# Macaron block, both gates: the normalization moves from VectorE to ScalarE, two batches ahead

## The reference

```python
x = x + 0.5 * ffn(layernorm(x))
x = x + attn(layernorm(x))
x = x + 0.5 * ffn(layernorm(x))

def ffn(x):                                   # E = 8 experts, K = 2
    logits = einsum('bsd,de->bse', x, gate_w) + gate_b
    probs = softmax(logits, axis=1)           # over the 512 tokens of a batch
    vals, idx = top_k(probs, 2)
    h = relu(x @ w1[e] + b1[e]); h = relu(h @ w2[e] + b2[e]); y = relu(h @ w3[e] + b3[e])
    v = einsum('ebso,bse->eo', y, w_tok)      # one vector for each expert
    return einsum('bse,eo->bso', indicator, v)
```

## Time and profile before

| | |
|---|---|
| median of 3 runs | 1137.03 us (1135.55 to 1138.68) |
| the profiled execution | 1137.88 us, of which the span from first to last instruction is 1136.1 us |
| PE busy | 1051.9 us, 93% of the span |
| DVE busy | 834.8 us, 73% |
| POOL busy | 696.8 us, 61% |
| ACT busy | 571.3 us, 50% |
| transfers | 59.35 MB, mean 52 GB/s |

### The profile page before, as it was taken

One profiled execution on the slowest core, in us unless ns is written; L12 is line 12 of the kernel. 1 busy time (PEld: TensorE's weight loads), 2 busy tenths in 40 slices (PEclk: granted clock), 3 DMA queues, 4 the chain that ended last, 5 costly groups with the idle time before them and its releaser, 6 DMA issues.

```text
span 1136.1 us, 15486 instructions
## 1 busy us (share of the span) xinstructions
PE 1051.9 (93%) x5687; PEld 636.9 (56%) x5687; DVE 834.8 (73%) x1078; ACT 571.3 (50%) x771; POOL 696.8 (61%) x367
## 2 busy tenths in 40 slices
PE   4599998679999999999999999999999976699996
PEld 1478886346555555555645654655654523588883
DVE  9979997757766766766766766776774464799994
ACT  3245555336554654644644654654564533255551
POOL 3435666357775776775785786686587662166552
PEclk8689999779999999999999999999999987699998
DMA  5143330000010011001001001001001112333312
GB/s 153 60 167 130 127 114 1 19 1 20 21 39 20 20 39 22 20 21 39 21 21 39 21 21 39 20 21 38 22 20 32 29 39 63 108 129 120 124 56 74
DMA packets 36336, 59.35 MB, mean 52 GB/s; under 512 B 10501, under 2 KB 23846, under 8 KB 36262
## 3 DMA queue, kind: packets, MB, share of 16 engines
q1 hardware_dynamic: 36262, 58.37, 17.0%
HBM read 55.20 MB, written 2.62 MB: 51 GB/s over the span
## 4 chain that ended last, share of the span: by engine, by line
PE 87%; DVE 9%; POOL 2%; issue 1%; ACT 1%; DMA 0%; SPq 0%; ACTq 0%; POOLq 0%; DVEq 0%
PE ring L745 19%; PE ring L516 8%; PE ring L510 8%; PE ring L512 8%; PE ring L698 6%; PE ring L716 5%; PE ring L722 5%; PE ring L718 5%; PE ring L720 5%; PE ring L755 5%; PE ring L731 3%; DVE xn L1048 2%; PE ring L680 2%; PE ring L655 1%; PE ring L681 1%; PE ring L682 1%
## 5 line engine op out<-in xcount | busy, mean ns | idle before, releaser
L1219 DVE TENSOR_REDUCE mx<-ring 128x2 f32<-128x1024 f32 x256 | 299.6, 1226 | 90.5 <-PE ring L698 90.5
L429 POOL TENSOR_TENSOR sum_picksT<-sum_picksT,P_wb 128x1024 f32<-128x1024 f32 x128 | 324.6, 2536 | 18.3
L916 ACT ACTIVATE P_wb<-ring 128x1024 f32<-128x1024 f32 x256 | 262.3, 1027 | 66.5 <-PE ring L722 38.2
L429 POOL TENSOR_TENSOR sum_picksT<-P_wb 128x1024 f32<-128x1024 f32 x64 | 153.9, 2404 | 175.0 <-ACT P_wb L916 175.0
L469 POOL TENSOR_TENSOR R<-t,R 128x512 fp32r<-128x512 f32 x128 | 163.6, 1300 | 145.5 <-ACT R L841 145.5
L745 PE MATMUL ring<-P_wb,t 128*64 128x512 f32 x1024 | 226.8, 595 | 0.0
L745 PEld LDWEIGHTS ring<-P_wb,t 128*64 128x64 f32 x1024 | 70.4, 137 | 133.0 <-issue 128.5
L836 ACT ACTIVATE t<-ring,bcol 128x512 f32<-128x512 f32 x128 | 81.4, 685 | 122.9 <-PE ring L516 120.0
L928 ACT COPY OZ<-ring 128x512 f32<-128x512 f32 x64 | 37.0, 588 | 198.8 <-PE ring L745 156.5
L698 PE MATMUL ring<-R 64*128 64x512 f32 x512 | 107.7, 416 | 6.0 <-DVE mx L1219 3.8
L510 PE MATMUL ring<-R,whi 128*128 128x512 f32 x320 | 105.8, 412 | 5.9 <-DVE ring L1160 3.2
(11 more groups left out here) (147 smaller groups left out, 1392.8 us busy)
## 6 DMA issues: line engine op xcount, KB each, us to landing
P_wb<-wd SPq DMA_DIRECT2D x64, 512.0 KB, 3.7
rzb_indp<-rzd SPq DMA_DIRECT2D x64, 256.0 KB, 3.9
xs<-in_L_attn_x SPq DMA_DIRECT2D x8, 256.0 KB, 3.8
zrc<-SZ SPq DMA_DIRECT2D x128, 2.0 KB, 1.7
out<-xs SPq DMA_DIRECT2D x8, 256.0 KB, 2.5
sum_picksT<-in_L_ffn_w SPq DMA_DIRECT2D x2, 512.0 KB, 5.3
MR<-mT SPq DMA_DIRECT2D x64, 4.0 KB
t<-in_L_ffn_w SPq DMA_DIRECT2D x1, 512.0 KB, 7.2
```

The lines of the kernel that those rows point to most:

```text
L429: pool.tensor_tensor(US[:, g % 2, c, :, :], first, PU[:, TPB * c + t, :, :], ALU.add).then_inc(s_ua, 1)
L916: act.activation(PU[:, u, :, :], ring[slot(("scores", g, u))][:, :, :], ACT.Exp, scale=SCALE).then_inc(s_exp, 1)
L1219: dve.tensor_reduce(mx[:, :, u], ring[slot(("max", g, u))][:, :, :], AX.X, ALU.max).then_inc(s_max, 1)
```

## The change

- DVE's `normal` goes to ACT: `Identity(scale * x + bias)` with `rstd` as scale and a new column `nmr` = -mean * rstd as bias, one instruction for a tile. In ACT's order the tiles of batch b+1 stand ahead of the two copies of batch b.
- `invert` gets one more small DVE operation, which writes `nmr`: six times in the program, twice in each gate and twice in attention, where `invert` is used too (for batch 0, and for batches 1 to 7).
- ACT rounds the three weight matrices into `whi`.
- POOL zeroes `MR`, ahead of its wait for the turned biases.
- Everything else stands as before. Attention's own `x_normal` stays on DVE.

```diff
+        nmr = sb("nmr", [P, NT])
...
@@ gpsimd
+            pool.memset(MR[:, :, :, :].rearrange("p g c s -> p (g c s)").bitcast(F32), 0.0).then_inc(s_mrz, 1)
             pool.wait_ge(s_bt, 1)
             pads()
             gate(0)
@@ scalar
             def gate(f):
                 s = F[f]
+                normals = [0]
+
+                def normal(b):
+                    act.wait_ge(s_nmr, (1 if b < TPB else 2) if f == 0 else (5 if b < B - 1 else 6))
+                    wait(act, s["xn_transposed"], b - 1)
+                    for j in range(TPB):
+                        t = TPB * b + j
+                        act.activation(xn[:, b % 2, j, :], xs[:, t, :], ACT.Identity, bias=nmr[:, t:t + 1],
+                                       scale=rstd[:, t:t + 1]).then_inc(s["xn_done"], 1)
+
                 for stage, arg in gate_steps(f):
                     if stage == "turn":
+                        for nb in range(normals[0], min(arg + 2, TPB if f == 0 and arg < TPB else (B - 1 if f and arg < B - 1 else B))):
+                            normal(nb)
+                            normals[0] = nb + 1
                         act.wait_ge(s["xn_transposed"], arg + 1)
...
+                    elif stage == "weights":
+                        act.wait_ge(s_wf, 64)
+                        act.copy(whi[:, arg, :, :].rearrange("p e o -> p (e o)"), wraw[arg]).then_inc(s_whd, 1)
@@ vector
             dve.memset(lgs, 0.0)
-            dve.memset(MR[:, :, :, :].rearrange("p g c s -> p (g c s)").bitcast(F32), 0.0)
             dve.memset(NEG[:, :].bitcast(F32), 0.0).then_inc(s_zero, 1)
...
             def invert(k):
                 dve.wait_ge(s_std, k + 1)
-                ln_link(dve.reciprocal(rstd[:, PARTS[k]], std[:, PARTS[k]]))
+                t = PARTS[k]
+                ln_link(dve.reciprocal(rstd[:, t], std[:, t]))
+                dve.scalar_tensor_tensor(out=nmr[:, t], in0=mean[:, t], scalar=-1.0, in1=rstd[:, t], op0=ALU.mult, op1=ALU.mult
+                                         ).then_inc(s_nmr, 1)
...
-                def normal(b):
-                    wait(dve, s["xn_transposed"], b - 1)
-                    for j in range(TPB):
-                        t = TPB * b + j
-                        dve.tensor_scalar(xn[:, b % 2, j, :], xs[:, t, :], mean[:, t:t + 1], rstd[:, t:t + 1],
-                                          ALU.subtract, ALU.mult).then_inc(s["xn_done"], 1)
...
-                    elif stage == "turn":
-                        normal(arg)
...
                     elif stage == "weights":
-                        dve.wait_ge(s_wf, 64)
-                        dve.tensor_copy(whi[:, arg, :, :].rearrange("p e o -> p (e o)"), wraw[arg]).then_inc(s_whd, 1)
                         if arg == 2:
```

More of the change, by code:

```diff
@@ L204, in macaron_kernel @@
         s_pads = sem("pads_zeroed")
+        s_nmr = sem("shift_ready")
+        s_mrz = sem("max_rows_zeroed")
         s_u, s_uc = sem("update_added"), sem("update_copied")
```

## The result

The changed kernel takes 1143.4 us (median of 4 runs, 1142.8 to 1144.9), and the kernel before 1137.3 us on the same chip (4 runs, 1135.6 to 1138.7): a ratio of 1.0065 with an interval of 1.0052 to 1.0078. **The change costs 0.65%**: that is 7.4 us (5.9 to 8.9). The medians lie 6.1 us apart, or 0.54%, within that interval. The profiled execution took 1142.83 us with a span of 1141.0 us, 4.9 us over the span before.

A forecast was written before the change was run, and what follows sets the result against it. PE carried 87% of the chain, but in the gates DVE was on it, slowed by POOL. Terms 3.0 + 0.75 + 1.2 - 0.1 + 0.2 = 5.05, rounded to 5.1 us, took the median from 1137.03 to 1142.1 us; range 1136.4 to 1146.5.

The forecast's parts named there:

- The tile on ACT: Both gates: one normalization on ACT lasts 0.48 us, 0.38 us from start to start in a row.
- The rival that it is free: Both gates: a column of scales costs nothing, 0.29 us a tile, 1136.5 us, no change; chance 0.15.
- deeper pipelining: Both gates: tiles in a row overlap more, below 0.30 us each, so the kernel gains, to 1133 us; chance 0.13.
- no overlap: Both gates: ACT's tile instructions do not overlap, 0.48 us a tile, +6.3 us, 1148.4 us; chance 0.06.
- In line with the copies: Second gate, batches 0 to 6: ACT's tiles and copies stand in line, 2.49 us a batch, +3.0 us.
- a wait for PE between batches: Gates: ACT was to have no other engine to wait for in steady state; such waits would make the prediction wrong.
- Batch 7: Second gate, last batch alone on the chain: `nmr` and four tiles take 1.62 us, not 1.11, +0.75 us.
- The first gate: First gate: ACT's last copy ends 2.0 us later, part is given back at POOL's subtractions, +1.2 us.
- The clock rival: Second gate: PE's clock stays at 1.2 GHz into the output projection, +4 to +7 us, 1146 to 1149 us; chance 0.06.
- what the cover gives back: End of first gate: DVE was waiting for POOL anyway, so a +2.0 us delay shrinks to +1.1, at most 1.4.
- The start, POOL's zeroing, the casts: Start of kernel and ACT's casts: statistics end earlier but POOL's paddings still hold DVE, casts cost nothing; -0.1, 0 to -0.5 us.
- `nmr` in attention: Attention's start: `nmr` for batch 0 stands between root and normalization, +0.2 us; hidden for batches 1 to 7.

The follow-up runs named there:

- e4: Changed kernel with scale=1.0 in place of the column `rstd` in ACT's tiles, so tokens are shifted and not scaled; 1138.5 us, 1.0017 of the kernel before.
- e1: Changed kernel with the first gate's normalizations back on DVE, the second gate's still on ACT; 1142.4 us, 1.0052 of the kernel before.
- e10: Changed kernel with `nmr` allocated behind all other tiles; 1144.8 us, 1.0068 of the kernel before.
- e2: Changed kernel with the second gate's normalizations back on DVE, the first gate's still on ACT; 1140.2 us, 1.0035 of the kernel before.
- e3: Changed kernel with every normalization on DVE and no `nmr` operation, keeping ACT's casts and POOL's memset; 1137.3 us, 1.0009 of the kernel before.
- e12: Changed kernel with all normalizations on DVE and `nmr` not allocated, keeping ACT's casts and POOL's memset; 1135.3 us, 0.9987 of the kernel before.

## Why the prediction was right, and where not

- **The tile on ACT** (0.48 us each, 0.38 from start to start): measured 0.484 and 0.387. e4 shows that the unknown part, the column of scales, costs 90 ns where 91 were taken. The rival that it is free falls, and so do those of deeper pipelining and of no overlap. The Trainium skill (ScalarE: Activation LUTs, What ACT_TABLE_LOAD costs), from whose figures the estimate of 0.386 us from tile to tile was worked out, agrees with the trace (0.387).
- **In line with the copies** (2.49 us a batch): measured 2.49. In the second gate +3.37 us where +3.0 was forecast: ACT worked from 926.44 to 944.34 us with one pause of 0.17, so 17.9 us where 17.55 were forecast; 28 tiles at 0.387 and not 0.38 us are 0.2 of the difference and the pause is the rest. The prediction had named a wait for PE between batches as a sign of being wrong. There was this one, of 0.17 us in seven batches, and e1 and e10 have it too: it needed a term, but it does not set the pace. e1 repeats the stretch to 0.01 us. Shown.
- **Batch 7** (+0.75): from the table load to PE's turn of the tiles 2.91 us before and 3.64 after, +0.73.
- **The first gate** (+1.2, with the start's -0.1): +2.52 in this pair. This term was mis-sized, in three steps. ACT's last copy ended at 35.5 us and not 33.9, mostly by the first: the second `nmr` was costed at 0.2 us and took 1.22, because it met POOL, though the prediction names this effect for three other operations, so ACT began the second root's tiles at 22.9 us and not 21.8:

```profile
20.31 2.51 POOL L456 TENSOR_TENSOR R<-OT_xnT,R 128x512 fp32r<-128x512 f32 x2 [1.23 <-ACT OT_xnT L876]
...
21.63 1.22 DVE L1053 SCALAR_TENSOR_TENSOR nmr<-mean,rstd 128x16 f32<-128x16 f32 x1
...
22.89 3.18 ACT L863 ACTIVATE xn<-xs,nmr,rstd 128x128 f32<-128x128 f32 x8 [1.58 <-DVE nmr L1053]
```

- The second step is PE's clock, to which the prediction gave no term in this gate. The turn of batch 7 took 1.11 us and not the 0.66 of full clock, and ACT waited 0.26 us for it. From the last copy to the successor of L1123 the forecast kept 3.0 us and it took 3.8, since the four logits took 2.98 us, and 2.02 at full clock, before and in the second gate. The stretches of the changed kernel, then of before (from:to, length, busy time and count of PE, PEld, DVE, ACT and POOL, the granted clock, DMA share, GB/s):

```profile
24.00:28.00 4.00, 2.24 (x10) 1.02 (x10) 0.39 (x3) 4.00 (x11) 0.90 (x1) 0.86 0.00 0
28.00:32.00 4.00, 3.41 (x7) 0.76 (x6) 0.00 (x0) 3.97 (x9) 1.63 (x2) 0.50 0.01 2
32.00:36.00 4.00, 3.29 (x10) 1.21 (x9) 0.00 (x0) 3.74 (x9) 1.73 (x2) 0.50 0.00 0
```

```profile
28.00:32.00 4.00, 3.26 (x12) 1.10 (x12) 4.00 (x11) 3.05 (x7) 1.44 (x2) 0.84 0.00 0
32.00:36.00 4.00, 2.87 (x19) 1.94 (x18) 3.33 (x5) 0.00 (x0) 4.00 (x3) 1.00 0.00 0
```

- From 28 us on ACT is busy nearly 4.00 of 4 us and DVE not at all, which is the mechanism in one row; and PE is still at 1.2 GHz (0.50) in a stretch in which it was back at 2.4 GHz (1.00) before. **The clock rival** was right in kind in the first gate, for about 1 us here, and wrong where it was placed, in the second gate: the clock came back later there too (0.50 at 930 to 934 us, 0.95 before), but behind ACT's pace that cost nothing, and it was at 1.00 when the projection began.
- The clock could cost more. In e2 and e10, which have the same tiles on ACT in the first gate, it stayed at 0.50 until past 40 us, and the product of W2 and b1 took 3.5 us and not 1.9. The changed kernel, then e10:

```profile
37.27 1.95 PE L610 MATMUL ring<-bcol,sum_picksT 128*128 128x1 f32 x16
```

```profile
36.99 3.58 PE L610 MATMUL ring<-bcol,sum_picksT 128*128 128x1 f32 x16
```

- The third step is what the cover gives back. The delay is +4.35 us at L1123's successor (39.25 against 34.90 us) and +2.5 at the gate's end, so 1.8 us came back, of which the forecast expected 0.9. The forecast was that POOL's third subtraction would hold L1079 or L1080 until 42.6 us. It ended at 43.95 us, as those two only began, and held neither: L1080 had taken 2.35 us before and takes 0.29 now (L1094), while the scaling of the probabilities, held by the second subtraction, went from 1.65 to 2.20 us (L1077).
- e2 and e10 show how much of this is chance. Both had L1123's successor at 40.61 us, +5.7 us. In e2 the scaling then took 0.49 us and the gate ended at 63.12, +2.63 us; in e10 it took 2.85 us and the gate ended at 65.50. That the first gate costs time on ACT is shown by the medians: e2 at +0.35% against e3 at +0.09% on the same chip, some 3 us with about 1.8 to each side. The 2.5 us of this pair of traces are one outcome of several.
- **The start, POOL's zeroing, the casts** (-0.1, 0 to -0.5): e3 is at +0.09% and e12 at -0.13%, both about nothing. The first root came at 10.35 us and not earlier than the 10.21 before, because two small operations (L1034, L1035) met POOL's paddings. The casts on ACT lay behind its last copy, as forecast.
- **`nmr` in attention** (+0.2): it took 0.16 us and cost nothing there. From batch 0's `rstd` to the end of its normalizations is 2.37 us before and 2.38 after.
- **Not forecast:** the two expert stages, +0.7 us each in the traces, of which 0.45 us by the placement of tiles.

So the mechanism, its place and the price of a tile were right, and the sum was somewhat small: 5.1 us against 5.9 to 8.9 by the ratio. In the traces the gates are +6.5 us and the placement twice 0.45: 7.4 us that the change brought. That this meets the ratio's 7.4 owes something to luck, as the first gate shows. The difference between the two spans is only 4.9 us, by attention and by PE's clock at the end of the expert stages, in the turn of the picks and in the output, none of it bound to the edits. The forecast's 1142.1 us lies 1.3 us below the median measured.

## What to carry to other kernels

Ask of work that is moved not how fast the new engine does it, but what it will stand in line with there. Here 0.48 us on ACT against a disturbed 0.57 on DVE looked level, but DVE's tiles lay beside ACT's copies and ACT's stand ahead of them: 4 x 0.39 + 0.95 us for a batch against 2.3. When two engines are both near a stage's pace, sharing the work so that both end together is the thing to try, with the work left whole on the faster one where it stands alone on the chain. Here that took the second gate from 17.6 us to 17.0, where the whole move took it to 21.1; the kernel as a whole ended 0.2% below the one before, of which the sharing's own part isn't shown.

## What the runs showed of the hardware

- **A DVE operation that meets POOL can be held for more than one POOL instruction.** The scaling of the probabilities took 0.49 us in e2, 0.93 in e3, 1.65 before, 2.20 after, 2.85 in e10 and 5.53 in e12, all started against the same three subtractions. Where it starts does not settle it alone: in e2 and e10 it started at 40.88 us, some 0.2 us before the second subtraction ended, and took 0.49 us in one and 2.85 in the other. After:

```profile
36.80 4.64 POOL L446 TENSOR_TENSOR wlo<-sum_picksT,whi 128x1024 fp32r<-128x1024 f32 x2
...
39.25 0.16 DVE L1133 TENSOR_TENSOR bcol<-bcol,ring 128x8 f32<-128x8 f32 x1 [14.87 <-PE ring L610]
...
39.52 2.20 DVE L1077 TENSOR_SCALAR P_wb<-P_wb,gst 128x512 f32<-128x512 f32 x1
...
41.41 2.54 POOL L446 TENSOR_TENSOR wlo<-t,whi 128x1024 fp32r<-128x1024 f32 x1
```

L1133 took 0.16 us in the midst of POOL's work; L1077 began 0.27 us later and ended at 41.7 us, 0.3 us behind POOL's second subtraction. That L1133 has only 8 columns is not what spared it: before, L1120 and L1121, also of 8 columns, took 1.27 and 1.31 us beside POOL, and 0.16 and 0.17 after. Those two read SBUF alone, and L1133 reads one of its two inputs from PSUM. The Trainium skill (GPSIMD Engine Reference, Key points) tells that POOL shares its SBUF interfaces with VectorE and that they contend for DVE instructions in a 2-port mode or with two SBUF inputs. L1133, with one SBUF input, agrees; that page gives no price, and here it was anything from nothing to 5 us for the same operation.
- **PE's clock in the first gate goes with the engine that writes its tiles.** With all tiles on ACT, two batches ahead, the granted clock was 0.50 from 28 to 36 us in all three executions (after, e2, e10). With the tiles on DVE or shared between the two it was 0.80 to 1.00 from 28 to 32 us and 0.99 or 1.00 from 32 to 36 us (before and eight others), and in e4, with the shorter tiles on ACT, 0.90 and 1.00.
- **Where tiles lie in SBUF moves the pace of an expert stage**: with 128 bytes of a partition more in front, the first 31 of its 32 sums take 125.9 us and not 125.4.
- **A column of scales costs as much as a column of biases**, 0.09 us each, on an ACT instruction of 128 columns.
